# A two-layer kernel on one core: attention steps in a fixed pattern of three experts a tile, the first shared-expert chunk ahead of the expert loop, and the experts' accumulators added by DMA onto the shared expert's rows

## What is computed

```python
# layer 0
xn  = layernorm(x)
att = attention(xn)          # 16 query heads that all equal the one value head; 1 key/value head of 128
ffn = experts(xn) + shared(xn)
#   experts: sigmoid router over 64 experts in 8 groups, the best 4 groups, top 8 of them,
#            weights divided by their sum, times 2.5; capacity 128 tokens an expert;
#            silu(x @ w_gate) * (x @ w_up) @ w_down with 88 hidden, scattered back and added
#   shared:  silu(x @ sh_gate) * (x @ sh_up) @ sh_down
x   = x + silu(ffn) * att
# layer 1
xn  = layernorm(x)
a1  = attention with 16 heads of 16 over the batch of two, causal
f1  = bitlinear(gelu(bitlinear(xn, w_fc)), w_proj)   # ternary weights
x   = x + silu(f1) * a1
```

## Time and profile before

| | |
|---|---|
| median of 3 runs | 421.01 us (420.65 to 421.41) |
| the profiled execution, its time | 421.63 us |
| its span in the trace | 419.9 us |
| mean granted TensorE clock | 0.942 |
| PE busy | 339.9 us, 81% |
| DVE busy | 312.6 us, 74% |
| ACT busy | 213.9 us, 51% |
| POOL busy | 234.6 us, 56% |
| data moved | 58.41 MB, 139 GB/s |

### The profile page before, as it was taken

The page is one execution under the profiler, slowest core; times in us unless marked ns, Lnnn a source line. Parts: engine busy times, 40 slices in busy tenths (PEclk is TensorE's granted clock), DMA queues, the critical chain, the costliest instruction groups (busy, mean ns, idle before and its releaser), DMA issues.

```text
span 419.9 us, 6972 instructions
## 1 busy us (share of the span) xinstructions
PE 339.9 (81%) x2044; PEld 256.6 (61%) x2044; DVE 312.6 (74%) x989; ACT 213.9 (51%) x540; POOL 234.6 (56%) x219
## 2 busy tenths in 40 slices
PE   0999649998976788989989898884078888988893
PEld 0984425665754656767867667652057767877772
DVE  4599744667899496849786886834669988899875
ACT  3754424334545244476446444411156788777781
POOL 3610072767767368777777787845166655663311
PEclk9999957999999799999999999987559999999999
DMA  8956941776767298988787787535910000000001
GB/s 262 382 183 201 352 139 39 166 151 136 175 152 180 66 258 187 253 220 221 171 190 172 166 187 154 91 46 84 311 54 2 25 2 26 27 27 25 9 21 51
DMA packets 34041, 58.41 MB, mean 139 GB/s; under 512 B 3835, under 2 KB 20563, under 8 KB 33875
## 3 DMA queue, kind: packets, MB, share of 16 engines
q1 hardware_dynamic: 21715, 39.08, 29.6%
q0 software_dynamic: 12288, 18.88, 24.4%
HBM read 40.22 MB, written 17.73 MB: 138 GB/s over the span
## 4 chain that ended last, share of the span: by engine, by line
PE 34%; DVE 22%; issue 17%; POOL 10%; ACT 8%; DMA 8%; POOLq 0%; DVEq 0%; ACTq 0%
DMA acc_d<-W,idxE 5%; POOL acc_d L498 4%; PE two L1451 4%; PE two L1714 4%; PE two L1590 3%; PE two L1403 3%; POOL W L479 2%; PE two L1556 2%; PE two L1461 2%; DVE W L1111 2%; DVE A L996 2%; PE two L1477 2%; POOL ny L544 2%; PE two L1413 2%; PE two L1681 2%
## 5 line engine op out<-in xcount | busy, mean ns | idle before, releaser
L498 POOL DMA_INDIRECT acc_d<-W,idxE x64 | 101.7, 1590 | 52.3 <-DVE W L1111 28.1
L479 POOL DMA_INDIRECT W<-tok_d,idxE x56 | 56.8, 1015 | 46.5 <-DVE idxE L1067 29.8
L710 ACT ACTIVATE W<-two 128x256 f32<-128x256 f32 x64 | 24.4, 381 | 75.4 <-PE two L1579 70.8
L1154 DVE SCALAR_TENSOR_TENSOR W<-W,two 128x88 f32<-128x88 f32 x64 | 15.4, 241 | 47.0 <-ACT W L726 42.2
L1714 PE MATMUL two<-W,A 128*128 128x257 f16 x256 | 30.0, 273 | 10.7 <-DVE F L1333 9.9
L686 ACT ACTIVATE A<-two 128x512 f16<-128x512 f32 x32 | 19.1, 597 | 31.7 <-PE two L1535 22.8
L1714 PEld LDWEIGHTS two<-W,A 128*128 128x128 f16 x256 | 24.0, 98 | 16.3 <-DVE F L1333 11.7
L1681 PE MATMUL two<-F,wfcT 128*128 128x256 f16 x256 | 32.5, 281 | 1.5 <-DVE F L1271 1.4
L797 ACT ACTIVATE two<-two,gwv 128x512 f32<-128x512 f32 x32 | 21.4, 668 | 23.9 <-PE two L1681 23.9
L1590 PE MATMUL two<-W 128*128 128x176 f32 x160 | 32.0, 324 | 0.0
L1556 PE MATMUL two<-A,v_hi 128*128 128x256 f16 x128 | 24.5, 296 | 9.1 <-DVE A L996 9.0
(11 more groups left out here) (240 smaller groups left out, 900.2 us busy)
## 6 DMA issues: line engine op xcount, KB each, us to landing
W<-in_gu SPq DMA_DIRECT2D x20, 352.0 KB
acc_d<-F SPq DMA_DIRECT2D x2, 2176.0 KB, 14.4
F<-in_gu SPq DMA_DIRECT2D x12, 352.0 KB
W<-in_dn SPq DMA_DIRECT2D x20, 176.0 KB
tok_d<-xr SPq DMA_DIRECT2D x2, 1280.0 KB, 5.9
F<-in_dn SPq DMA_DIRECT2D x12, 176.0 KB
x<-in_q SPq DMA_DIRECT2D x4, 512.0 KB, 6.7
A<-in_Wo SPq DMA_DIRECT2D x1, 2048.0 KB, 12.4
```

What stands on the lines that cost most here:

```text
L479: pool.indirect_dma_start(out=xg[n % XR], out_offset=None, in_=tok_d[:, :], in_offset=bass.IndirectOffsetOnAxis(ap=idxE[:, n:n + 1], axis=0))\
L498: pool.indirect_dma_start(out=acc_d[n % 2][:, :], out_offset=bass.IndirectOffsetOnAxis(ap=idxE[:, n:n + 1], axis=0), in_=ysb[n % YS], in_o ...
L710: sc.activation(xgT[n % 2], bk_(2)[:, 0:D].rearrange("p (k n) -> p k n", k=KH), ACT.Copy)\
```

## The change

1. A tile of attention has three steps instead of four, and expert n in 15 to 62 has exactly one: step 0 is the first half of the probabilities and the next tile's scores, step 1 the next tile's exponentials and the second half, step 2 attend on odd tiles and the projected tiles on even ones. The first scores move one expert forward. The tables of other work move by one to three experts.
2. The first chunk of the shared expert is computed by PE ahead of the loop. One of four head sums is taken before the loop, two at expert 0 and one at expert 17.
3. tot is xn: POOL adds both accumulators onto the shared expert's rows by DMA (add_acc). The second add of a pair waits for the first to land. The loads by SP, acc1, total, add_shared and first_total go.

```diff
-STEPS = 4
-START, END = 15, 62
+STEPS = 3
+START = 15
-SUM_AT, TERN_AT = 34, (37, 39, 42, 44, 47, 49, 52, 54)
+SUM_AT, TERN_AT = 34, (37, 38, 40, 43, 44, 46, 49, 52)
...
-UP_AT = {0: (0, 0), 1: (0, 1), 3: (1, 0), 4: (1, 1), 6: (2, 0), 7: (2, 1), 9: (3, 0), 10: (3, 1)}
-GATE_AT = {2: 0, 5: 1, 8: 2, 11: 3}
+UP_AT = {3: (1, 0), 4: (1, 1), 6: (2, 0), 7: (2, 1), 9: (3, 0), 10: (3, 1)}
+GATE_AT = {1: 0, 5: 1, 8: 2, 11: 3}
...
-HEADS_AT = (16, 18, 20, 21)
-PICK_AT, DEN_AT, WEIGH_AT = 6, 19, (22, 23, 25, 27)
+HEADS_AT = {0: (1, 2), 17: (3,)}
+PICK_AT, DEN_AT, WEIGH_AT = 6, 20, (22, 25, 26, 28)
...
-    done, now = [min(max(m - START, 0) * BESIDE // (END - START), BESIDE) for m in (n, n + 1)]
-    return [(k // STEPS, k % STEPS) for k in range(done, now)]
+    return [divmod(n - START, STEPS)] if START <= n < START + NT * STEPS else []
...
-        tot = W[:, 0:4096].rearrange("p (t d) -> p t d", t=NT)
+        tot = xn
...
-            def total(p):
+            def add_acc(i, p):
+
+                if p == 0:
+                    pool.wait_ge(y_added[i], 16 * (NE // 2))
+                if i == 0:
+                    pool.wait_ge(weighed, NT // 4)
+                else:
+                    pool.wait_ge(acc_ld[p], 16)
+                pool.dma_start(pair(tot, p), acc_v[i][:, 0:NT, :].rearrange("p (s i) d -> p s i d", s=2)[:, :, p, :],
+                               accum_op=ALU.add).then_inc(acc_ld[p], 16)
...
+            for i in range(2):
+                for p in range(2):
+                    add_acc(i, p)
             for p in range(-AHEAD, NP):
                 if p >= 0:
                     weigh(p)
                 if 1 < p + AHEAD < NP:
-                    if p < 0:
-                        total(p + AHEAD)
-                        add_shared(p + AHEAD)
                     gated(p + AHEAD)
-                if 0 <= p and p + 1 + AHEAD < NP:
-                    total(p + 1 + AHEAD)
                 if p >= -2:
                     roots(p)
-                if p == -1:
-                    total(p + 1 + AHEAD)
-                if -1 <= p and p + 1 + AHEAD < NP:
-                    pool.wait_ge(own_ready, p + 2)
-                    add_shared(p + 1 + AHEAD)
+                if p == -AHEAD:
+                    for i in range(2):
+                        add_acc(i, 2)
+                        add_acc(i, 3)
                 if 0 < p + AHEAD < NP:
                     add_gated(p + AHEAD)
+                if -1 <= p and p + 2 + AHEAD < NP:
+                    add_acc(0, p + 2 + AHEAD)
+                    add_acc(1, p + 2 + AHEAD)
                 if 0 <= p < LAST:
                     finish(p)
...
             def slots(g):
 
                 pe.wait_ge(hot_ready, g + 1)
+                if g:
+                    pe.wait_ge(idxE_ready, g)
...
             pe.wait_ge(ld_sh, 2 * 16)
+            shared_up(0, 0)
+            shared_up(0, 1)
```

More of the change, by code:

```diff
@@ L292, in build @@
             "sc_ps", "nmax_ready", "probs_ready", "pT_ps", "pT_hi_ready", "pT_lo_ready", "o_ps", "oT_ready", "wo_ps", "s0_ready")]
[L293 to L294 removed]
+        gated_ready, gate_ready, silu_ready, x1_ready, xh_ready, xT1_ps, xT_hi_ready, xT_lo_ready = [
+            sem(n) for n in ("gated_ready", "gate_ready", "silu_ready", "x1_ready", "xh_ready", "xT1_ps",
                              "xT_hi_ready", "xT_lo_ready")]
@@ L392, in _ @@
                     sp.dma_start(wpo4_s[:, cols], wpo4[:, cols]).then_inc(ld_w2, 16)
[L394 to L408, removed]
             for p in range(NP):
@@ L501, in _ @@
                     .then_inc(y_added[n % 2], 16)
-            def total(p):
[L505 to L510, removed]
+            def add_acc(i, p):
[7 more added lines that the diff above has]
+                               accum_op=ALU.add).then_inc(acc_ld[p], 16)
             def gated(p):
                 pool.wait_ge(s0_ready, NT)
-                pool.wait_ge(acc_ready, p - 1)
+                pool.wait_ge(acc_ld[p], 32)
                 pool.tensor_tensor(pair(s0, p), pair(s0, p), pair(tot, p), ALU.mult).then_inc(gated_ready, 1)
@@ L696, in attention_step @@
                 if step == 0:
+                    if t % 2 == 0 and t:
+                        take_oT(t // 2 - 1)
                     high_probs(t, 0)
                 elif step == 1:
-                    if t % 2 == 0 and t:
-                        take_oT(t // 2 - 1)
-                elif step == 2:
+                    if t + 1 < NT:
+                        exps(t + 1)
                     high_probs(t, 1)
-                elif t + 1 < NT:
-                    exps(t + 1)
             def turn(n):
@@ L1001, in attention_step @@
                     low_probs(t, 0)
-                    if t % 2 and t > 1:
-                        take_projected(t - 2)
-                elif step == 1:
                     if t + 1 < NT:
                         top(t + 1)
-                elif step == 2:
+                elif step == 1:
                     low_probs(t, 1)
-                elif step == 3:
                     ve.wait_ge(probs_ready, t + 1)
@@ L1013, in attention_step @@
                     then(ve.reciprocal(rinv[:, t:t + 1], rsum[:, t:t + 1]))
-                    if t % 2 == 0 and t:
-                        take_projected(t - 2)
+                elif t % 2 == 0 and t:
+                    take_projected(t - 2)
+                    take_projected(t - 1)
             def flat_g(a):
@@ L1102, in shared_weighed @@
                 for t in range(t0, t1):
-                    last = mark(ve.tensor_scalar(xn[:, t, :], xn[:, t, :], den[:, t:t + 1], None, ALU.mult))
-                ve.wait_ge(dve, last)
+                    ins = ve.tensor_scalar(xn[:, t, :], xn[:, t, :], den[:, t:t + 1], None, ALU.mult)
+                ins.then_inc(weighed, 1)
             def put(n):
@@ L1160, in _ @@
                     shared_product(PRODUCT_AT[n])
+                if n in TAKE_AT:
+                    take_indices(TAKE_AT[n])
                 if n in HOT_AT:
@@ L1170, in _ @@
                     weights_sum()
-                if n in HEADS_AT:
-                    head_sum(HEADS_AT.index(n))
+                for i in HEADS_AT.get(n, ()):
+                    head_sum(i)
                 if n in WEIGH_AT:
                     shared_weighed(4 * WEIGH_AT.index(n), 4 * WEIGH_AT.index(n) + 4)
-                if n == START - 1:
+                if n == START - 2:
                     top(0)
@@ L1207, in newton, with first_gated @@
                 then(ve.scalar_tensor_tensor(out=y, in0=t_, scalar=1.5, in1=y, op0=ALU.add, op1=ALU.mult))
-            def first_total(p):
+            def first_gated(p):
                 ve.wait_ge(acc_ld[p], 32)
-                then(ve.tensor_tensor(pair(tot, p), pair(tot, p), pair(acc1, p), ALU.add))
-                ve.tensor_tensor(pair(tot, p), pair(tot, p), pair(xn, p), ALU.add).then_inc(tot_first, 1)
-            def first_gated(p):
-                ve.wait_ge(tot_first, p + 1)
                 then(ve.tensor_tensor(pair(s0, p), pair(s0, p), pair(tot, p), ALU.mult))
```

32 lines of the change are left out of this document (11 added, 21 removed).

## The result

The changed kernel takes 429.6 us (median of 4 runs, 425.9 to 431.4) against 420.9 us beside it: ratio 1.019, 95% interval 1.013 to 1.026. It is slower, by 8.7 us; 422.5 was forecast. Its profiled execution took 430.1 us, with a span of 428.1 against 419.9, and the 8.2 us between the spans can be followed event by event. The events are starts of single instructions in the two traces; the last column is what the difference gained or lost since the event above it.

A forecast was written before the change was run, and what follows sets the result against it. POOL's queue was taken to bound the expert loop and POOL's order the second layer's rounds. Loop -17, hand-off +2.8, rounds +15.5 gave +1.3, rounded to +1.5 on 421.0: 422.5 us, own range 418.5 to 427, whole range 411 to 435.

The forecast's parts named there:

- The rounds: Second layer, pairs 4 to 7: POOL's wait for a landing delays weigh, 4.2 us a round, 15.5 in all.
- X: POOL's own time to issue one accumulating DMA of 256 rows: taken as 1.2 us, from 1.0 to 3.2.
- L: Time of an accumulating DMA from start to landing: taken as 4.1 us, from 3.0 to 6.2.
- The half microsecond taken as absorbed: In each lengthened round, 4.7 us longer, half a microsecond absorbed since PE is busy 11.39 of 13.0.
- The hand-off: Last scatter to first root: eight issues, two waits delay the root 4 us; +2.8 net, bounds -1 and +8.
- Experts 15 to 24: Expert loop: removing DVE's pile at experts 18 to 21 gives 3.4 instead of 4.2 us an expert, -7.
- 24 to 56: Expert loop near POOL's queue floor of 3.18 us an expert: at most 4.1 us to be had, 2 taken.
- The end: Scatters of experts 56 to 63 and the landing: 19.4 us possible instead of 22.7, 2.5 of the 3.3 taken.
- The start: First shared chunk's matmuls moved ahead of the loop, under the wait for the gather: gain 5.5 us, bounds 3.5 and 7.5.
- tables one expert earlier: Part of the loop's fixed pattern with moved head sums; its 7 us gain was given for nine experts, 15 to 24.
- Rival 2: The expert loop gives little, some 9 us, as POOL's floor and landing waits stay: 430.5 us, chance 0.14.
- Rivals 1 and 3: Accumulate cheap and the loop's gain stands, 414 us, chance 0.32; accumulate dear, L + X of 8, 436 us, chance 0.10.

The follow-up runs named there:

- one half alone: Two kernels: the kernel before with only the change's expert-loop edits, 409.3 us, and with only its accumulator adds by DMA, 440.5 us.
- the earlier accumulate: The changed kernel with the first accumulate of a pair issued one round ahead of the second in the rounds; 417.4 us, ratio 0.993 to the kernel before.
- the pattern alone: The kernel before with only the three-step tile pattern; shared chunk, slot lists, head sums and weights keep their old places; 416.9 us, ratio 0.991.
- the loop half alone: The kernel before with three-step tiles, first shared chunk ahead and moved tables; accumulators loaded and added as before; 409.3 us, ratio 0.974.
- the kernel with the slot lists back: The loop half alone, but with the slot lists of experts 48 to 63 built at experts 13 to 19 again, not 12 to 18; 409.3 us, ratio 0.972.
- the PE-filled kernel: The changed kernel with 30 useless identity transposes ahead of the attention's transposes in rounds 0 to 3, where PE idles; 431.7 us, ratio 1.026.
- the three edits to it: Made singly to the loop half alone: slot lists back, 409.3 us; first shared chunk back inside the loop, 412.9; head sums moved later, 411.4.
- two of them together: The loop half alone with both the slot lists back at experts 13 to 19 and the head sums later; 410.2 us, ratio 0.975.
- the accumulates behind the roots: The changed kernel with the rounds' accumulates issued after the roots, the first of a pair a round earlier; 417.5 us, ratio 0.994.

## Why the prediction was right and where it was not

*The rounds*: forecast 4.2 a round after the first, 15.5 in all; measured 3.9 to 4.3 after the first, 15.5. The order on POOL's queue, with its cover of 1.6 us, was the right way to read it, and the experiments with one half alone and with the earlier accumulate show it. X was taken as 1.2 and is 1.20 to 1.22; L was taken as 4.1 and the time from the first start to the second as L + 0.7 = 4.8, which is 4.53 to 4.67. The half microsecond taken as absorbed, for PE's idle time, is there, but the reason given is not shown: from add_gated to PE's transposes it is 9.05 us and not 9.5, and the rest of the round takes 7.9 and not 8.2.

*The hand-off*: root forecast 4 late, measured 4.0; half of the removed 2.5 us of adds given back, measured 1.2. The eight issues in the queue were counted rightly, and end at 297.1 where the same count from this loop's end gives 296.4 (306.1 less 9.7).

*Experts 15 to 24*: forecast -7, measured -6.8 in this trace and -4.3 to -7.6 in the five traces of this loop. The prediction did not say how much of it the pattern alone would do; it does 3.2 us.

*24 to 56*: forecast -2, measured -0.8; the loop comes near its floor of 3.18 us an expert and does not reach it (3.29 measured, 3.31 before). *The end*: -2.5, measured -3.0.

*The start* is the step that failed. Forecast -5.5 up to expert 15, measured +0.9. The first scatter is 4.5 early, but from there to expert 15 it takes 60.2 us and not the 54.8 of before, a stretch whose change the sum had at nothing. 3.4 of these 5.4 us are TensorE's clock, which fell in two places in this trace and in that of the loop half alone; the other three traces of this loop have 56.9. The 2.1 that stay are as much as the hole before the scatter of expert 14 adds at the full clock; the kernel with the slot lists back puts 1.0 us down to the tables. The prediction's "tables one expert earlier" stood in the heading of a part whose gain was then given for experts 15 to 24 only, and the first scores one expert forward had no price at all.

But a loss at expert 15 is not a loss at the end, nor a gain a gain: with scatter 15 anywhere from 123.34 to 127.11 us the new loop's last scatter stands at 277.8 to 279.3. What the sum did wrong is therefore wider than the hole. It priced the loop region by region and added up. From the first scatter to the last it had 7 + 2 + 2.5 = 11.5 us; the traces of the new loop show 209.3 to 212.4 us against 217.5 and 217.7, so 5.1 to 8.4. The medians say the same: of the 11.3 us that the loop half alone wins, the chunk makes 3.7 (5.5 forecast) and the rest some 7.4 (11.5 forecast), of which the pattern alone 3.2. What takes an early lead back between expert 15 and the end is not shown. It isn't POOL's queue at its floor, for such a queue would keep a lead: from the first scatter to that of expert 56 there are 56 pairs of 3.18 us, 178 us, and the loop half alone takes 195 against 198.7 before.

*The sum*: -17 + 2.8 + 15.5 forecast, -9.7 + 2.8 + 15.5 measured; the sign is right, the size missed by the loop's 7.3 us. The range of 411 to 435 held the result because it had been drawn around the rivals; the forecast's own range ended at 427. The table's last line is 8.6 and the span's difference 8.2. Rival 2 (the loop gives some 9) had the term right with 0.14; its 430.5 is the nearest of the four. Rivals 1 and 3 fell with L + X: it is 5.0 to 5.2 (the start of the second less 0.7, plus 1.2), where 5.3 was forecast. The estimate by the Trainium skill's page "DMA: Bandwidth & Descriptors" (its anatomy of one DMA), 2.6 us for 256 KB, is well below what these accumulates took, 4.5 us by the changed kernel's page of the profile from issue to landing; the trace decides, and it was right not to take it.

The clock fell to 0.81 to 0.90 in the lengthened rounds, which the prediction had named as a danger. Against the rounds of the PE-filled kernel at 1.00 it cost 0.6 us in the one at 0.81 and nothing in the others, so it did not make them dearer by much.

The kernel with the loop half alone beats both: 409.3 us. None of the three edits to it, nor two of them together, was measurably better.

## What to carry to other kernels

Read the queue of the engine that issues a DMA: a wait for a landing holds back all that is queued behind it, and the price is the landing less the cover of the first thing queued that another engine needs; busy shares show nothing of it. If an accumulate must follow another on the same bytes, issue the first one early enough that the second finds it landed. Price a change of a loop from one start to one end, not region by region: a lead won in one region may be gone in the next, and a piece that is moved meets other work at its new place. Before reading two or three microseconds out of one trace, look at other traces of kernels that have this stretch in common.

## What the runs showed of the hardware that was not expected

A plain accumulating DMA of 256 rows of 1 KB costs POOL 1.20 us, less than the 1.59 of the indirect one with 128 rows, and lands 4.5 us after its issue (median, 16 of them; 4.5 to 5.0 in the other kernels that have them).

The granted clock can differ between executions in the same stretch of the same code. In the changed kernel it is 0.61 from 115 to 119 us, and 16 products take 3.53 us; with the same loop in the kernel with the earlier accumulate it is 1.00, and they take 1.92. PE had waited 2.42 us just before in both.

DVE's instructions take longer while POOL issues DMAs. In the kernel with the accumulates behind the roots, DVE's two normalising instructions meet two issues (POOL at 333.12 for 2.47 us) and take 1.33 us in all; in the kernel before, with no issue beside them, they take 0.73. DVE's timelines of the two kernels:

```profile
333.92 1.33 DVE L1236 TENSOR_SCALAR F<-x,mv,ny 128x256 f32<-128x256 f32 x2
```

```profile
352.77 0.73 DVE L1261 TENSOR_SCALAR F<-x,mv,ny 128x256 f32<-128x256 f32 x2
```

In the rounds before and after, beside other issues, they take 0.80 and 0.84. DVE is busy 12.5 us in this round against 11.8, about the 0.7 by which it is too long; the first round is 0.6 too long with only 0.80 there, so that sum is not shown in full. With the earlier accumulate DVE is busy 12.9 and 12.8 us in the two rounds of 14 us. The Trainium skill's page "SBUF — State Buffer" tells, in its box on DVE blocking DMA, of a DVE instruction that keeps POOL from writing descriptors, and in its section "Who interferes with whom" that the engine that issues first holds the shared ports for its whole instruction while the other waits. Here it is DVE that gives way. That the shared port is the cause was not tried apart.

The landing of the same DMA differs between kernels and rounds, 4.5 to 6.1 us from start to the next one's start, without other traffic than the output's stores, and the rounds follow it one for one. Whether it makes the spread of the changed kernel's runs, 425.9 to 431.4 us, is not shown: the kernel before has no such DMA and spreads as widely, 417.5 to 423.5.
